# First head of an attention kernel: a second projection on TensorE in place of a copy by DMA, and the value and weight work moved into its first step

## The reference

```python
q = jnp.einsum('bim,mhd->bhid', x, wq)
k = jnp.einsum('bim,mhd->bhid', x, wk)
v = jnp.einsum('bim,mhd->bhid', x, wv)
q = rope(q); k = rope(k)   # [even*cos - odd*sin, even*sin + odd*cos], halves of 64
s = jnp.einsum('bhid,bhjd->bhij', q, k) / 128
s = s - 1e30 * (i < j)     # causal
p = softmax(s)
o = jnp.einsum('bhij,bhjd->bhid', p, v)
return jnp.einsum('bhid,hdm->bim', o, wo)
```

## Time and profile before

| | us |
|---|---|
| median of 3 runs | 1674.55 |
| lowest, highest run | 1670.38, 1675.01 |
| the profiled execution | 1672.75 |
| its span | 1670.7 |
| busy in the span: PE, DVE, ACT, POOL | 1625.1, 1244.0, 1214.0, 1413.7 |

### The profile page before, as it was taken

One profiled execution on the slowest core, in us unless ns is written; L12 is line 12 of the kernel. 1 busy time (PEld: TensorE's weight loads), 2 busy tenths in 40 slices (PEclk: granted clock), 3 DMA queues, 4 the chain that ended last, 5 costly groups with the idle time before them and its releaser, 6 DMA issues. The chain is left out here.

```text
span 1670.7 us, 29885 instructions
## 1 busy us (share of the span) xinstructions
PE 1625.1 (97%) x10452; PEld 1471.7 (88%) x10452; DVE 1244.0 (74%) x2899; ACT 1214.0 (73%) x2427; POOL 1413.7 (85%) x797
## 2 busy tenths in 40 slices
PE   4999999999999999999999999999999997999997
PEld 4899999999999999999999999999999986999997
DVE  5787778777877777778777877787777777677775
ACT  3877777777777777777777777777777764665664
POOL 4799989998999899998999899989998975777884
PEclk8999999999999999999999999999999999999999
DMA  5222232223222322232223222322232323123212
GB/s 151 77 76 75 77 99 71 74 75 98 74 75 74 100 73 75 74 99 76 77 77 102 77 77 77 102 77 76 77 89 76 89 77 102 45 67 96 68 33 58
DMA packets 69763, 134.10 MB, mean 80 GB/s; under 512 B 19312, under 2 KB 38000, under 8 KB 69616
## 3 DMA queue, kind: packets, MB, share of 16 engines
q1 hardware_dynamic: 67856, 130.10, 28.9%
q10 hardware_dynamic: 1760, 2.10, 0.4%
HBM read 56.36 MB, written 8.70 MB: 39 GB/s over the span
## 5 line engine op out<-in xcount | busy, mean ns | idle before, releaser
L506 ACT ACTIVATE probs<-ps_slot,neg_max 128x640 f32<-128x640 f32 (+7 forms) x512 | 381.1, 746 | 154.2 <-DVE neg_max L649 154.2
L649 DVE CUSTOM_DVE_ANT_0 ps_slot<-ps_slot,causal 128x640 f32<-128x640 f32 (+7 forms) x512 | 383.0, 769 | 132.7 <-PE ps_slot L57 132.4
L904 PE MATMUL ps_turn<-ident,probs 128*128 128x128 f32 x2048 | 279.2, 274 | 2.3 <-DVE pt_high L676 1.2
L55 PE MATMUL ps_slot<-k,q 128*128 128x512 f32 (+4 forms) x768 | 274.9, 358 | 6.5 <-DVE v L694 5.1
L57 PE MATMUL ps_slot<-k,q 128*128 128x512 f32 (+4 forms) x768 | 264.9, 345 | 0.0
L56 PE MATMUL ps_slot<-k,q 128*128 128x512 f32 (+4 forms) x768 | 263.1, 343 | 0.0
L904 PEld LDWEIGHTS ps_turn<-ident,probs 128*128 128x128 f32 x2048 | 232.8, 140 | 21.8 <-issue 2.1
L676 DVE TENSOR_TENSOR pt_split<-ps_turn,pt_split 128x512 fp32r<-128x512 f32 x256 | 175.3, 685 | 93.4 <-ACT pt_split L551 93.4
L439 POOL TENSOR_TENSOR q<-rot_q,q 128x1024 fp32r<-128x1024 f32 x63 | 152.2, 2416 | 52.6 <-ACT q L534 52.6
L423 POOL TENSOR_TENSOR swapped_k<-swapped_k,rope 128x1024 f32<-128x1024 f32 x63 | 152.4, 2420 | 42.6 <-DMA swapped_k<-unrot_k 42.5
L417 POOL TENSOR_TENSOR rot_k<-unrot_k,rope 128x1024 f32<-128x1024 f32 x64 | 154.7, 2417 | 16.4 <-ACT unrot_k L516 13.8
(11 more groups left out here) (198 smaller groups left out, 4426.1 us busy)
## 6 DMA issues: line engine op xcount, KB each, us to landing
swapped_k<-unrot_k SPq DMA_DIRECT2D x128, 256.0 KB, 3.6
swapped_q<-unrot_q SPq DMA_DIRECT2D x128, 256.0 KB, 3.6
inv_b<-inv_rows SPq DMA_DIRECT2D x64, 512.0 KB, 4.7
y_t<-y_sum SPq DMA_DIRECT2D x8, 512.0 KB, 5.4
x_raw<-y_t SPq DMA_DIRECT2D x8, 512.0 KB, 4.1
unrot_q<-in_L_attn_x SPq DMA_DIRECT2D x8, 512.0 KB, 5.4
row_b<-r_rows SPq DMA_DIRECT2D x16, 256.0 KB, 3.6
x_raw<-x_cols SPq DMA_DIRECT2D x7, 512.0 KB, 5.3
```

The costliest lines, as they stand in the source:

```text
L55: pe.matmul(out, stat_hi, mov_hi, start=start, stop=False, skip_group_check=True)
L506: act.activation(probs_tile(t), score_tile(name, head, i), ACT.Exp, scale=-1.0, bias=neg_max[:, head.par, t:t + 1], accum_out=sums[:, head ...
L649: dve.tensor_tensor_reduce(tile, tile, causal[:, T - WIDTH[t]:T], -1.0, UNSEEN, ALU.add, ALU.min, neg_max[:, head.par, t:t + 1]).then_inc( ...
L904: last = pe.transpose(bank[:, at:at + P], probs_tile(t)[:, j * P:(j + 1) * P], ident[:, :])
```

## The change

For head 0 the swap is no longer a DMA. wk and wq of head 0 are also loaded with their two halves of 64 columns exchanged: the first heads' weights now lie 64 columns into their buffer, and a small DMA puts columns 64 to 127 of head 0 ahead of them, so that the first 128 columns are the crossed weights. They are split as well (ACT, then DVE, in `pt_split`), and PE projects x with them into `both_turn` (k) and `both_y` (q): 12 more matmuls. DVE multiplies these sums by sin' straight out of PSUM, and q's sums by cos, so that `raw_q`, both swaps and POOL's sin' product of the first head are gone.

Around it: SP loads the rope tables without waiting for x. ACT runs one small Exp ahead of everything (its table load with it), makes the hi halves of x before it issues wv, wo and the rest, and the rest of wk and wq goes to `y_head` and `y_sum`. PE first makes 28 transposes of the identity matrix. The wv*wo product goes to the slot that k of head 0 had; k and q of head 1 go to `both_turn` and `both_y`. The two value portions, `raw_q` and `mul_cos_q` of head 1, and the lo halves of the other weights move into step 0, among its scores. POOL starts its steps only when lo of q of head 0 is made.

```diff
@@ sync
-            sp.wait_ge(first_x_landed[1], 16)
             for i, table in enumerate((rope_c, rope_s)):
                 sp.dma_start(kept.rope[:, i, :], table).then_inc(rope_landed[i], 16)
-            first = Head(0, 0, heads)
-            swap(1, first)
-            swap(0, first)
             steps(sp, step, 16)
@@ gpsimd
+            pool.sem_inc(raw_made[0], 2)
             first = Head(0, 0, heads)
             pool.wait_ge(rope_landed[0], 16)
             mul_cos_k(first)
             pool.wait_ge(rope_landed[1], 16)
-            mul_sin(0, first)
+            pool.wait_ge(lo_made[0], 1)
             steps(pool, step, 16)
@@ scalar
-            act.wait_ge(first_x_landed[1], 16)
-            act.dma_start(w_raw["v"], ...)
-            act.dma_start(w_raw["o"], ...)
             for n, w in (("k", wk), ("q", wq)):
-                act.dma_start(w_raw[n][:, FIRST_HEADS * D:], ...)
+                act.dma_start(w_raw[n][:, 0:D // 2], w[:, 0, D // 2:D]).then_inc(crossed_landed, 16)
+            act.wait_ge(consts, 1)
+            act.activation(inv[:, 0, :], kept.minus_half[:, :], ACT.Exp)
             for half in range(2):
                 act.wait_ge(first_x_landed[half], 16)
                 act.activation(kept.x_t[0][:, 0, half_cols(half)], ...)
+            act.dma_start(w_raw["v"], ...)
+            act.dma_start(w_raw["o"], ...)
+            for n, w in (("k", wk), ("q", wq)):
+                act.dma_start(rest_raw[n][:, 0:(H - FIRST_HEADS) * D], ...)
+            act.wait_ge(crossed_landed, 32)
+            for which, n, scale in ((1, "k", 1.0), (0, "q", 1.0 / P)):
+                act.wait_ge(w_landed[n], 16)
+                act.activation(crossed[which][0], w_crossed[n], ACT.Copy, scale=scale).then_inc(crossed_hi, 1)
             raw_k(first)
-            raw_q(first)
-            act.wait_ge(wvo_made, 1)
-            act.activation(wvo_part(0), both_y, ACT.Copy).then_inc(wvo_hi, 1)
-            split_hi(1, first)
-            raw_k(second)
-            split_v_hi(first.step(-2))
-            split_hi(0, first)
-            split_v_hi(first.step(-1))
-            raw_q(second)
             split_rest_hi("k", WK_HI, 1.0)
             split_rest_hi("q", WQ_HI, 1.0 / P)
+            act.wait_ge(cos_made[1], 1)
+            raw_k(second)
+            split_hi(1, first)
+            split_hi(0, first)
+            act.wait_ge(wvo_made, 1)
+            act.activation(wvo_part(0), slot("k", first), ACT.Copy).then_inc(wvo_hi, 1)
@@ scalar, step 0: behind exp s4: raw_q(after), exp s7, split_v_hi(-2); behind exp s5: split_v_hi(-1)
@@ vector
+            split_crossed_lo(0, 1, "k", 1.0)
+            split_crossed_lo(1, 0, "q", 1.0 / P)
+            first_sin_k()
             dve.wait_ge(rope_landed[0], 16)
-            mul_cos_q(first)
-            first_sin_k()
+            first_cos_sin_q()
             first_add(1)
-            dve.wait_ge(wvo_hi, 1)
-            dve.tensor_tensor(wvo_part(1), both_y, ...)
             first_add(0)
             first_split_lo(1)
-            split_v_lo(first.step(-2))
             first_split_lo(0)
-            split_v_lo(first.step(-1))
-            mul_cos_q(second)
-            split_rest_lo("k", WK_HI, WK_LO, 1.0)
-            split_rest_lo("q", WQ_HI, WQ_LO, 1.0 / P)
+            dve.wait_ge(wvo_hi, 1)
+            dve.tensor_tensor(wvo_part(1), slot("k", first), ...)
@@ vector, step 0: behind rowmax s4: mul_cos_q(after); behind rowmax s7: split_rest_lo k, split_v_lo(-2);
@@                  behind rowmax s5: split_rest_lo q; behind turn 6b, ahead of rowmax s10: split_v_lo(-1)
+            def first_cos_sin_q():
+                for place, half in enumerate((1, 0)):
+                    cols = half_cols(half)
+                    dve.wait_ge(filled["q"], place + 1)
+                    dve.tensor_tensor(rot[0][:, cols], slot("q", first)[:, cols], kept.rope[:, 0, cols], ALU.mult)...
+                    dve.wait_ge(crossed_filled, place + 2)
+                    last = dve.tensor_tensor(swapped[0][:, cols], both_y[:, cols], kept.rope[:, 1, cols], ALU.mult)
+                last.then_inc(sin_made[0], 1)
@@ tensor
+            pe.wait_ge(consts, 4)
+            for i in range(28):
+                pe.transpose(both_turn[:, i % 8 * P:(i % 8 + 1) * P], ident[:, :], ident[:, :])
             ...  # project k of head 0
+            pe.wait_ge(crossed_lo, 1)
+            for half in range(2):
+                last = project_crossed(1, half, both_turn)
+            last.then_inc(crossed_filled, 1)
             pe.wait_ge(w_lo["q"], 1)
-            project_q(first, 1)
-            project_q(first, 0)
+            pe.wait_ge(crossed_lo, 2)
+            for half in (1, 0):
+                project_q(first, half)
+                project_crossed(0, half, both_y).then_inc(crossed_filled, 1)
+            pe.wait_ge(sin_made[1], 1)
+            project_k(second)
             ...  # wv*wo, now behind raw_made[1] and into slot("k", first)
-            pe.wait_ge(cos_made[0], 2)
-            pe.wait_ge(raw_made[0], 2)
-            project_k(second)
-            pe.wait_ge(raw_made[1], 1)
+            pe.wait_ge(sin_made[0], 1)
             project_q(second, 1)
             project_q(second, 0)
-            pe.wait_ge(wvo_lo, 1)
-            project_v(first.step(-2))
-            project_v(first.step(-1))
@@ tensor, step 0: wait wvo_lo ahead of scores s7; behind s7 wait raw_made[0], cos_made[0], project_v(-2);
@@                  behind scores s5 wait v_lo, project_v(-1)
```

More of the change, by code:

```diff
@@ L216, in attention_block @@
         w_raw = {n: probs[:, i * H * P:(i + 1) * H * P] for i, n in enumerate("qkvo")}
+        rest_raw = {"k": y_head, "q": y_sum}
+        w_first = {n: w_raw[n][:, D // 2:D // 2 + FIRST_HEADS * D] for n in "kq"}
+        w_crossed = {n: w_raw[n][:, 0:D] for n in "kq"}
+        crossed = [[pt_split[:, part, i, 0:D] for part in range(2)] for i in range(2)]
         consts = s.sem("consts")
@@ L263, in slot @@
             place, step = SLOT_FILLS[name]
+            if name in "kq" and head.number() == 1:
+                return both_turn if name == "k" else both_y
             return ps_slot[:, (head.at + step + place) % 2, :]
@@ L269, in v_sums @@
                 return slot("v", head)
-            return (both_turn, both_y)[head.number() + 2]
+            return both_y
         def score_tile(name, head, i):
@@ L421, in mul_sin @@
                     return
-                pool.wait_ge(swap_landed[which], head.made() * 32)
+                pool.wait_ge(swap_landed[which], head.number() * 32)
                 pool.tensor_tensor(swapped[which][:, :], swapped[which][:, :], kept.rope[:, 1, :],
@@ L618, in step @@
                 exp("s4", head)
+                if is_step(head, 0):
+                    raw_q(after)
+                    exp("s7", head)
+                    split_v_hi(head.step(-2))
                 turn("3", before)
@@ L623, in step @@
                     act.activation(kept.z_t[:, 0, :], z_slot, ACT.Copy).then_inc(z_hi, 1)
-                exp("s7", head)
+                if not is_step(head, 0):
+                    exp("s7", head)
                 for half in range(2):
@@ L632, in step @@
                 exp("s5", head)
+                if is_step(head, 0):
+                    split_v_hi(before)
                 exp("s10", head, 1)
@@ L736, in step @@
                 rowmax("s4", head)
+                if is_step(head, 0):
+                    mul_cos_q(after)
                 turn("5a", before)
@@ L744, in step @@
                 rowmax("s7", head)
+                if is_step(head, 0):
+                    split_rest_lo("k", WK_HI, WK_LO, 1.0)
+                    split_v_lo(head.step(-2))
                 turn("3", before)
@@ L854, in project_half, with project_crossed @@
                 return matmul_split(pe, slot("qk"[which], head)[:, cols], w[:, hi, :], w[:, lo, :],
+                                    xt[:, 0, cols], xt[:, 1, cols], True, True)
+            def project_crossed(which, half, out):
+                xt, cols = kept.x_t[0], half_cols(half)
+                return matmul_split(pe, out[:, cols], crossed[which][0], crossed[which][1],
                                     xt[:, 0, cols], xt[:, 1, cols], True, True)
@@ L981, in step @@
                 turn("7a", before, ("5b", before))
+                if is_step(head, 1):
+                    pe.wait_ge(v_lo, 2)
                 weigh_high(before, (0, 1))
-                free_slot(v_lo, before, -2, -2, 2)
+                if not is_step(head, 0):
+                    free_slot(v_lo, before, -2, -2, 2)
                 if is_step(head, 1):
@@ L1011, in step @@
                 weigh_high(before, (2, 3))
-                if after.live():
+                if is_step(head, 0):
+                    pe.wait_ge(wvo_lo, 1)
+                elif after.live():
                     pe.wait_ge(raw_made[0], after.made() * 2)
@@ L1015, in step @@
                 scores("s7", head)
```

(7 more changed lines are left out.)

55 lines of the change are left out of this document (34 added, 21 removed).

## The result

| | before | after |
|---|---|---|
| median of the runs, us | 1674.38 (5 runs, 1670.38 to 1675.01) | 1663.51 (5 runs, 1662.31 to 1665.19) |
| the profiled execution | 1672.75 | 1663.51 |
| its span | 1670.7 | 1661.4 |
| s4 of head 0 starts | 31.39 | 20.64 |
| its row maximum | 36.51 | 21.91 |

The ratio of the times is 0.9945, with a 95% interval of 0.9935 to 0.9956, or 7.4 to 10.9 us. The kernel is faster, by 10.9 us between these medians and by 9.2 between the profiled executions, though by only half a percent of its time. 1665.5 was predicted. (In the kernel before, the last reciprocal of the attention is at 1381.41, so the last head's work ends later than the 1379 said ahead.)

A forecast was written before the change was run, and what follows sets the result against it. It took PE as busy without a gap from s32 of head 0, so only that start counted: 47.71 - 39.4 = 8.3 off 1672.75 gives 1664.4, or 1666.2 against the median; predicted 1665.5, range 1660.0 to 1671.0.

The forecast's parts named there:

- The stream up to s32: Start of head 0: s4 at 20.05 us, maximum of s10 8.3 earlier, s32 at 39.4 instead of 47.71.
- ACT's issues: ACT's start: hi of x ends about 6.0, four DMAs to 9.0, then crossed weights' hi, 0.3; their load costs nothing.
- Transposes: PE's start: 28 transposes from 2.4 us at 0.2, later 0.1, ending near 7.6 (bounds 5.2 to 13.6).
- Rest of the weights: Load of the rest of wk and wq, which ACT waits for: landed at 13.0 us, bounds 12 and 16.9.
- lo halves of the rest: DVE in step 0, after the maximum of s7: 1.65 us, half of 3.31, for the rest of k's weights.
- Second projection: Head 0's start: crossed k at 9.65 to 11.05 us; 12 added matmuls, 2.8 us, hide in DVE's 6.2.
- the swap was hidden anyway: Rival at head 0's start: s4 would start as before, time 1672.75; nothing gained, chance 0.04.
- Rivals: Clock falls (0.15), loads late (0.10), step 0 gives back or keeps more (0.11), nothing gained (0.04), slower (0.05).
- the rest of the weights took 1.7 us more: Rival in step 0: DVE's and ACT's added work overlaps worse, gain 5 to 6, 1667 to 1668; chance 0.11 including more kept.
- The rival of the clock: PE's clock falls in step 0; a 3 to 4.4 us stretch from s32 loses 1.5 to 2.2, 1666.5 to 1668; chance 0.15.
- wrong if a window behind s32 has a clock of 0.5: Sign against the forecast, beside s4 after 23 us or PE gaps behind s32; PE should be busy throughout from 39.4.
- the second value portion stands ahead of the maxima of s10: Step 0: ACT's 1.05 and DVE's 1.2 in sequence add 2.3 us before the maxima of s10.

The follow-up runs named there:

- no_warm: The changed kernel without the 28 transposes ahead of the first projection; median 1665.46 us, ratio to the kernel before 0.9948.
- best: lo_late plus ACT's hi halves of the other heads' weights moved behind the hi half of wv*wo; median 1660.96 us, ratio to the kernel before 0.9925.
- dma_swap: The changed kernel with head 0's halves exchanged by two DMAs again, no crossed weights or second projection; median 1672.34 us, ratio to the kernel before 0.9988.
- swap_quiet: dma_swap with wv, wo and the rest of wk and wq loaded only after both swaps landed; 1674.54 us, one run.
- rest_early: The changed kernel with DVE's lo halves of the other heads' weights back ahead of step 0; median 1669.36 us, ratio to the kernel before 0.9978.
- fill: The changed kernel with 14 identity transposes where PE waits ahead of s32; median 1664.33 us, repeated 1663.64; ratio to the kernel before 0.9941.
- before_again: The kernel before, unchanged, run once more for its trace; 1673.28 us, one run.
- lo_late: The changed kernel with DVE's maxima of s10 ahead of the second value portion's lo half; median 1662.52 us, repeated 1661.85; ratio to the kernel before 0.9929.
- act_first: The kernel before with only ACT's order changed: early table load, hi of x before its DMA issues; median 1671.74 us, ratio to the kernel before 0.9985.
- after_again: The changed kernel run once more, with nothing changed; median 1664.73 us, ratio to the kernel before 0.9945.

## Why the prediction was right, point by point

**The stream up to s32 was right.** The times were 20.64 for s4 (20.05 predicted), 37.54 for the maximum of s10 (37.45) and 39.27 for s32 (39.4); the gain at s32 is 8.44, where 8.3 was the sum. Some of that agreement is luck, since terms offset each other:

- *ACT's issues.* The crossed weights' hi was put at 9.0, behind four DMA issues. The issues ended at 7.81; what ACT waited for then, 0.8 us more, was the load of the crossed weights. The prediction had priced that load at nothing. It landed 6.4 us after an issue at 2.13, so even with ACT's issues ending at 9.0, as laid out, it would have been only 0.5 us ahead. The four loads of the start, from the view of DMA issues (the last number is the median from issue to landing):

```profile
probs<-in_L_attn_wk ACTq DMA_DIRECT2D x1, 128.0 KB, 3.8
probs<-in_L_attn_wq ACTq DMA_DIRECT2D x1, 128.0 KB, 4.3
probs<-in_L_attn_wk ACTq DMA_DIRECT2D x1, 32.0 KB, 5.6
probs<-in_L_attn_wq ACTq DMA_DIRECT2D x1, 32.0 KB, 6.4
```

  A quarter of the bytes, in rows of 256 and issued behind the larger ones, took 2 us longer to land. The Trainium skill, "DMA: Bandwidth & Descriptors", Specifications, asks for 512 bytes a row. The trace would fit that, but other loads were in the queue ahead of them, and no run parts the two causes.
- *Transposes.* Done at 7.08 (7.6 taken; the prediction's own figures, 22 at 0.2 and 6 at 0.1, give 7.4), 0.166 us each on average. no_warm shows that lateness here gets through to s4 and s32 alike, 0.7 us of the 1.5 by which DVE's sin product was late.
- *Rest of the weights.* Landed at 14.55, not 13.0; 1.06 us of DVE's waiting ahead of lo k comes from there, inside the bounds. best took 0.8 of it away.
- *lo halves of the rest.* The first took 2.57 us, beside POOL, and not 1.65. All but 0.1 of the difference was hidden, since ACT's hi of the values, which DVE needs next, ended only at 28.48.
- *Second projection.* It carries more than half of the gain, by dma_swap; "the swap was hidden anyway" is false by 4.8 us at s4 and 4.9 to 5.5 at s32.
- *Rivals.* Two were priced loosely. If the rest of the weights took 1.7 us more, a gain of 6.6 is left, not 5 to 6, and the times of the rivals start partly from 1672.75 and partly from the median. (In step 0 the entries listed up to the maximum of s7 add up to 24.2, not 24.4.)

**The rival of the clock came true, beside the forecast.** By the prediction's own sign, "wrong if a window behind s32 has a clock of 0.5", its account of what follows s32 failed: the window says 0.54. The rival said 1.5 to 2.2 us for a stretch behind s32; the traces say 1.6 (9.45 less 7.86). Another 0.3 us from s32 to the reciprocal is there even at the full clock (7.84 to 7.91 without the stretch, against 7.56 to 7.59 in the kernel before), where the prediction had the change add nothing; its cause was not looked for. The rival was given 0.15, and its time 1666.5 to 1668, yet the medians are 1663.51 and 1664.73.

The stretch is not rare: it lies behind s32 also in dma_swap, swap_quiet and rest_early (clocks of 0.57 to 0.63 over the 4 to 4.6 us from there, and 9.26 to 9.46 us to the reciprocal), so in five of the six traces of kernels in which the maxima of s10 stand behind the second value portion and nothing fills PE's wait, all but no_warm. That it is missing in more of the executions without a profile would fit a median for fill no lower than after's, but no run shows it.

Why the time still came out below the rival's has two parts that the traces show. The attention ends 7.0 us earlier (means of two: 1381.98 and 1374.95) and the feed-forward part was 1.2 us shorter, together 8.2 between the spans; both intervals of the ratio, 7.4 to 10.9 us and 7.0 to 11.2, hold that. And the first trace of the kernel before, from which the sum was taken, was one of its quieter executions: its clock over the whole span was 0.995, and 40 of the 44 later runs of that kernel show 0.992 to 0.994. before_again, at 0.993, has s32 1.1 us later. Counted from that trace, the gain at s32 is 9.0 to 9.6 us.

**The forecast of the time** rested on 1672.75, put up by about half of the 1.8 to the median. The sum on the profiled execution was 1664.4, and it came to 1663.51: the low stretch took 1.6 us, and a short feed-forward part, 2.55, gave more back. That the two nearly cancel is luck.

**A step that was right but not seen as a choice.** The prediction wrote down that the second value portion stands ahead of the maxima of s10, and put its price at 2.3 us. lo_late got 2.05 back by moving two lines: most of it was not a cost of moving the work, but of its place in DVE's stream.

## What to carry to other kernels

Where one engine is busy without a gap from some instruction on, forecast that instruction's start: lay out the streams with durations from rows, and price a small DIRECT2D load from issue to landing even when it seems covered. Put work that is moved into waits behind what the bound engine waits for next, in each engine's own order. A reordering that frees an engine earlier may give little while a DMA copy stands behind it, since the copy then meets the loads (4.2 us became 1.2 in act_first). Before two traces are compared, look at where each has its low clock: here the way from s4 to s32 differed by 0.5 and 0.9 us between two executions of one kernel, with the low stretches in other places.

## What the runs showed of the hardware

- The stretches at the low clock are 3.5 to 4 us long near s32 and do not stay in place: 39.3 to 43.0 and 41.0 to 44.8 in two executions of one kernel, 36.0 to 39.8 without the first transposes, none behind s32 with 14 transposes ahead of it, and none up to 60 us in lo_late, where s32 comes 2.4 us earlier. Earlier ones move as well: 25 to 30 and 20 to 25 us in the two traces of the kernel after. In the kernel after, PE had been busy for 2.34 of the 5.30 us before the fall, at a granted clock of 1.00.
- The clock column can miss a low level at the very start. In no_warm it says 1.00 for 7.0 to 9.6 us, while the 512-column matmuls there step at 0.43 us, as they do elsewhere at 0.50 to 0.53 (act_first, after_again).
- A swap of 512 KB (two DMAs of 256 KB) within the chip's on-chip memory took 4.45 us from issue to use with no load beside it, 6.0 and 7.4 beside 1.8 MB of loads.
- DVE's scalar_tensor_tensor of 128x768 took 2.27, 2.57 and 3.10 us beside POOL, and half of 3.31 in the trace before, where POOL was idle for half of the time.
